# Attention's first group in small pieces: rows in two DMAs ahead of the weights, tiles from VectorE, rounding by halves

## What is computed

```python
def _layernorm(x, eps=1e-05):
    return (x - mean(x)) / sqrt(var(x) + eps)
def _rmsnorm(x, gamma):
    return x / max(norm(x), 1e-12) * 256 ** 0.5 * gamma
h = _rmsnorm(_layernorm(x), gamma)
q, kv, a = split(einsum('bnd,ed->bne', h, w_qkva), 3)    # w_qkva: 768 x 256
a = sigmoid(a)
y[t] = a[t] * y[t-1] + kv[t]                              # along the 1024 rows of a batch
x = x + q * y
x = x + moe(_layernorm(x))
```

## Time and profile before

| | us |
|---|---|
| median of 3 runs | 1058.49 |
| lowest, highest | 1057.33, 1059.9 |
| profiled execution, own time | 1060.74 |
| its span | 1059.0 |
| TensorE busy | 1011.7 (96%) |
| VectorE busy | 634.9 (60%) |
| ScalarE busy | 522.9 (49%) |
| GpSimd busy | 504.9 (48%) |

### The profile page before, as it was taken

The page is one execution under the profiler, slowest core; times in us unless marked ns, Lnnn a source line. Parts: engine busy times, 40 slices in busy tenths (PEclk is TensorE's granted clock), DMA queues, the critical chain, the costliest instruction groups (busy, mean ns, idle before and its releaser), DMA issues.

```text
span 1059.0 us, 20091 instructions
## 1 busy us (share of the span) xinstructions
PE 1011.7 (96%) x7277; PEld 955.5 (90%) x7277; DVE 634.9 (60%) x1094; ACT 522.9 (49%) x783; POOL 504.9 (48%) x285
## 2 busy tenths in 40 slices
PE   6999997999797699999999999999999999999998
PEld 5788997999797599999999999999999999999997
DVE  5997688775231365555555656555565556476766
ACT  3555431322131266666666766666666667423232
POOL 2226200000042277878787787878778776500000
PEclk9999998999898899999999999999999999999999
DMA  8333304004557567777777777777777777244231
GB/s 300 88 85 95 81 2 139 12 10 167 193 196 267 182 228 254 262 222 254 233 253 241 256 228 263 244 243 254 221 258 230 251 228 249 76 137 140 79 119 40
DMA packets 162219, 192.72 MB, mean 182 GB/s; under 512 B 76281, under 2 KB 147458, under 8 KB 151938
## 3 DMA queue, kind: packets, MB, share of 16 engines
q1 hardware_dynamic: 154656, 173.04, 50.4%
q0 software_dynamic: 6720, 18.36, 5.6%
q10 hardware_dynamic: 802, 0.79, 0.2%
HBM read 165.42 MB, written 26.74 MB: 181 GB/s over the span
## 4 chain that ended last, share of the span: by engine, by line
PE 86%; DVE 7%; DMA 3%; issue 2%; ACT 1%; POOL 0%; SPq 0%; DVEq 0%; POOLq 0%
PE ps L939 49%; PE ps L954 16%; PE ps L958 8%; PE ps L980 4%; PE ps L849 3%; PE ps L987 2%; DVE y_sb L1096 2%; PE ps L835 1%; DMA sorted_rows<-x_stage 1%; DVE hT_lo L1056 1%; DMA x_stage<-z_rows,idx_x 1%; PE ps L914 1%; PE ps L860 1%; DVE stats L1036 1%; DMA resid<-in_L_attn_x_dram 0%
## 5 line engine op out<-in xcount | busy, mean ns | idle before, releaser
L939 PE MATMUL ps<-xs_hi,w_both 128*128 128x256 f32 x3072 | 566.0, 284 | 8.3 <-DVE h_early L1378 7.5
L939 PEld LDWEIGHTS ps<-xs_hi,w_both 128*128 128x128 f32 x3072 | 480.6, 190 | 11.2 <-DVE h_early L1378 7.9
L939 PE MATMUL ps<-xs_lo,w_both 128*128 128x256 f32 x1536 | 435.8, 284 | 0.0
L551 POOL TENSOR_TENSOR w_both<-raw,w_both 128x2048 fp32r<-128x2048 f32 x65 | 307.9, 4737 | 94.2 <-ACT w_both L692 85.8
L939 PEld LDWEIGHTS ps<-xs_lo,w_both 128*128 128x128 f32 x1536 | 291.4, 190 | 0.1
L954 PE MATMUL ps<-w_both,h_hi 128*128 128x512 f32 x768 | 275.6, 401 | 6.7 <-DVE h_lo L1383 6.7
L958 PE MATMUL ps<-w_both,h_lo 128*128 128x256 f32 x768 | 216.6, 282 | 0.0
L733 ACT ACTIVATE silu<-ps 128x512 f32<-128x512 f32 x192 | 114.3, 595 | 205.3 <-PE ps L939 205.3
L1378 DVE TENSOR_TENSOR ps<-ps,silu 128x512 f32<-128x512 f32 x164 | 114.7, 699 | 127.1 <-ACT silu L733 120.2
L692 ACT ACTIVATE w_both<-raw 128x1024 fp32r<-128x1024 f32 x186 | 186.3, 1051 | 4.1 <-DMA raw<-in_L_ffn_w_up_dram 2.3
L954 PEld LDWEIGHTS ps<-w_both,h_hi 128*128 128x128 f32 x768 | 145.5, 189 | 40.9 <-DVE h_lo L1383 7.3
(11 more groups left out here) (184 smaller groups left out, 791.0 us busy)
## 6 DMA issues: line engine op xcount, KB each, us to landing
raw<-in_L_ffn_w_up_dram SPq DMA_DIRECT2D x33, 1024.0 KB, 5.3
raw<-in_L_ffn_w_gate_dram SPq DMA_DIRECT2D x33, 1024.0 KB, 6.9
raw<-in_L_ffn_w_down_dram SPq DMA_DIRECT2D x33, 1024.0 KB, 5.6
sorted_rows<-x_stage SPq DMA_DIRECT2D x32, 256.0 KB, 2.2
x_rows<-sorted_rows SPq DMA_DIRECT2D x128, 64.0 KB, 5.2
got<-expert_rows SPq DMA_DIRECT2D x32, 256.0 KB, 3.4
resid<-in_L_attn_x_dram SPq DMA_DIRECT2D x8, 512.0 KB, 6.6
z_rows<-z_all SPq DMA_DIRECT2D x8, 512.0 KB, 2.9
```

The lines of the kernel that those rows point to most:

```text
L551: pool.tensor_tensor(w_lo[buf][:, k, :], source[:, k, :], w_hi[buf][:, k, :].bitcast(F32), ALU.subtract).then_inc(wlo_ready[k], 1)
L939: last = pe.matmul(o, w[:, part, at[kd]:at[kd] + P], xx[:, u, kd, :], start=i == 0, stop=i == len(terms) - 1)
```

## The change

All of it lies before and in group 0 of attention.

- SP issues x of group 0 in two halves (two tiles each, `x_half`), then the weights in three parts (`w_in`, in the order 2, 1, 0), then x of groups 1 to 7 without a wait. ScalarE's queue keeps gamma and the router rows.
- TensorE does 14 of the warming transposes first, as soon as the identity is there, and 4 before the projection. In between it turns gamma and router, weight part 2, the four tiles of group 0 one by one as they come (`turn_first`), weight parts 1 and 0.
- GpSimd makes only the scales of group 0, no bias. VectorE makes the tiles of group 0 itself (`first_rows`: minus mean, times scale). 
- ScalarE does the first two steps of `prepare` for parts 2 and 1 (times gamma in two halves, rounding); VectorE keeps the subtraction (`prepare_lo`) and all of part 0.
- ScalarE rounds group 0's turned rows in two halves and VectorE makes their rests in two halves (`first_lo`); the first projection waits for the first half, and for the second only at its fourth term.
- VectorE takes group 1's `bn_stats` (`collect1`) before these and the `bn_aggr` and variances (`settle1`) after them.

The core of the diff:

```diff
@@ sync @@
-            for g in range(NC):
+            for half in range(2):
+                ts = slice(half * CT // 2, (half + 1) * CT // 2)
+                sp.dma_start(resid[:, ts, :], x_t[:, ts, :]).then_inc(x_half[half], 16)
+            w_v = w_qkva.rearrange("(e p) d -> p e d", p=P)
+            for part in PARTS:
+                es = slice(part * KD, (part + 1) * KD)
+                sp.dma_start(w_nat[:, es, :], w_v[:, es, :]).then_inc(w_in[part], 16)
+            for g in range(1, NC):
                 sp.dma_start(resid[:, g * CT:(g + 1) * CT, :], x_t[:, g * CT:(g + 1) * CT, :]
                              ).then_inc(x_in[g], 16)
-                if g == 0:
-                    sp.wait_ge(small_in, 48)
@@ gpsimd @@
                 pool.wait_ge(mv1_ready, g + 1)
+                if g == 0:
+                    pool.tensor_tensor(scale1[:, ts], var1[:, ts], power[:, :], ALU.pow).then_inc(scaled1, 1)
+                    return
@@ scalar @@
-            h_rows(0)
+            def prepare(nth, part):
+                if nth == 0:
+                    act.wait_ge(prep_done, 1)
+                act.wait_ge(prep, nth + 2)
+                for k in range(KD):
+                    last = act.activation(wT_32[:, part, k, :], ps[:, PART_BANKS[nth], k * D:(k + 1) * D],
+                                          ACT.Identity, scale=gT[:, k:k + 1])
+                last.then_inc(wT_scaled, 1)
+                act.wait_ge(wT_scaled, nth + 1)
+                act.activation(wT_hi[:, part, :, :], wT_32[:, part, :, :], ACT.Copy).then_inc(wT_rounded, 1)
...
-            h_hi_part(0)
+            prepare(0, PARTS[0])
+            act.wait_ge(hT_psum, 1)
+            act.activation(hT_hi[:, 0, 0, :], ps[:, 4, :], ACT.Copy).then_inc(hT_first_hi, 1)
+            act.activation(hT_hi[:, 0, 1, :], ps[:, 5, :], ACT.Copy).then_inc(hT_rounded, 1)
+            prepare(1, PARTS[1])
             h_rows(1)
@@ tensor @@
-            pe.wait_ge(small_in, 48)
+            for _ in range(WARM[0]):
+                pe.transpose(ps[:, 3, 0:P], ident[:, :], ident[:, :])
+            pe.wait_ge(small_in, 32)
...
+            def turn_first():
+                for k in range(CT):
+                    pe.wait_ge(h_first, k + 1)
+                    for kd in range(KD):
+                        last = pe.transpose(ps[:, 4 + kd, k * P:(k + 1) * P],
+                                            z_all[:, k, kd * P:(kd + 1) * P], ident[:, :])
+                last.then_inc(hT_psum, 1)
...
+                        if first and e == 0 and i == len(terms) // KD:
+                            pe.wait_ge(hT_split, 1)
...
-            turn_h(0)
-
-            for _ in range(WARM):
+            turn_w(PARTS[0], PART_BANKS[0])
+            turn_first()
+            turn_w(PARTS[1], PART_BANKS[1])
+            turn_w(PARTS[2], PART_BANKS[2])
+            for _ in range(WARM[1]):
                 pe.transpose(ps[:, 3, 0:P], ident[:, :], ident[:, :])
@@ vector @@
+            def first_rows():
+
+                dve.wait_ge(scaled1, 1)
+                for t in range(CT):
+                    dve.tensor_scalar(z_all[:, t, :], resid[:, t, :], mv1[:, t, 0:1], scale1[:, t:t + 1],
+                                      ALU.subtract, ALU.mult).then_inc(h_first, 1)
+
+            def first_lo(kd, rounded, signal):
+
+                dve.wait_ge(rounded, 1)
+                dve.tensor_tensor(hT_lo[:, 0, kd, :], ps[:, 4 + kd, :], hT_hi[:, 0, kd, :].bitcast(F32),
+                                  ALU.subtract).then_inc(signal, 1)
...
             dve.wait_ge(prep_done, 1)
-            prepare(0, PARTS[0])
-            prepare(1, PARTS[1])
-            h_lo_part(0)
-            statistics1(1)
+            first_rows()
+            collect1(1)
+            prepare_lo(0, PARTS[0])
+            first_lo(0, hT_first_hi, hT_first_lo)
+            first_lo(1, hT_rounded, hT_split)
+            settle1(1)
+            prepare_lo(1, PARTS[1])
             prepare(2, PARTS[2])
             statistics1(2)
```

More of the change, by code:

```diff
@@ L215, in preln_scan_moe_kernel @@
         x_in = [sem(f"x_in{g}") for g in range(NC)]
+        x_half = [sem("x_half0"), sem("x_half1")]
+        w_in = [sem(f"w_in{part}") for part in range(3)]
+        h_first = sem("h_first")
+        hT_first_hi, hT_first_lo = sem("hT_first_hi"), sem("hT_first_lo")
+        wT_scaled = sem("wT_scaled")
         small_in = sem("small_in")
@@ L224, in preln_scan_moe_kernel @@
         prep_done = sem("prep_done")
-        wT_made = sem("wT_made")
         wT_rounded = sem("wT_rounded")
@@ L284, in preln_scan_moe_kernel @@
         PART_BANKS = (0, 1, 6)
-        WARM = 18
+        WARM = (14, 4)
         R0 = SA + NS
@@ L619, in _ @@
             for k, (dst, src) in enumerate((
-                    (w_nat[:, :, :], w_qkva.rearrange("(e p) d -> p e d", p=P)),
                     (g_nat[:, :], gamma.rearrange("(k p) -> k p", p=P)),
@@ L798, in _, with turn_w @@
             last.then_inc(prep, 1)
-            for part, bank in zip(PARTS, PART_BANKS):
+            def turn_w(part, bank):
+                pe.wait_ge(w_in[part], 16)
                 for k in range(KD):
@@ L838, in route, with project @@
                 last.then_inc(lg_psum, 1)
-            def project(g, part, bank, signal):
+            def project(g, part, bank, signal, first=False):
                 c = g % 2
@@ L871, in _ @@
                 two = 6 - one
-                pe.wait_ge(hT_split, g + 1)
-                if g >= 1:
+                if g == 0:
+                    pe.wait_ge(hT_first_lo, 1)
+                    pe.wait_ge(wT_split, 1)
+                else:
+                    pe.wait_ge(hT_split, g + 1)
                     pe.wait_ge(y_ready, g)
-                if g == 0:
-                    pe.wait_ge(wT_split, 1)
-                project(g, 2, one, a_psum)
+                project(g, 2, one, a_psum, first=g == 0)
                 if g >= 1:
@@ L1030, in _, with collect @@
             step(dve.memset(keep[:, :, 0:1], 0.0))
-            def statistics(g, stats, mv, signal):
+            def collect(g, stats, signal):
                 if g >= 1:
@@ L1035, in statistics, with settle @@
                 for k in range(CT):
+                    if signal is mv1_taken and g == 0 and k % 2 == 0:
+                        dve.wait_ge(x_half[k // 2], 16)
                     last = dve.bn_stats(stats[:, k, :], resid[:, g * CT + k, :])
                 step(last)
+            def settle(g, stats, mv, signal):
                 for k in range(CT):
@@ L1041, in statistics, with collect1, settle1 @@
                 dve.wait_ge(signal, g + 1)
-            def statistics1(g):
-                dve.wait_ge(x_in[g], 16)
-                statistics(g, stats1, mv1, mv1_taken)
+            def statistics(g, stats, mv, signal):
+                collect(g, stats, signal)
+                settle(g, stats, mv, signal)
+            def collect1(g):
+                if g >= 1:
+                    dve.wait_ge(x_in[g], 16)
+                collect(g, stats1, mv1_taken)
+            def settle1(g):
+                settle(g, stats1, mv1, mv1_taken)
                 ts = slice(g * CT, (g + 1) * CT)
@@ L1051, in statistics1 @@
                                   ).then_inc(mv1_ready, 1)
+            def statistics1(g):
+                collect1(g)
+                settle1(g)
+            def first_rows():
[7 more added lines that the diff above has]
+                                  ALU.subtract).then_inc(signal, 1)
             def h_lo_part(g):
@@ L1129, in x_lo, with prepare_lo @@
                                   xs_hi[:, par, :, :].bitcast(F32), ALU.subtract).then_inc(x_split, 1)
+            def prepare_lo(nth, part):
+                dve.wait_ge(wT_rounded, nth + 1)
+                dve.tensor_tensor(wT_lo[:, part, :, :], wT_32[:, part, :, :],
+                                  wT_hi[:, part, :, :].bitcast(F32), ALU.subtract).then_inc(wT_split, 1)
             def prepare(nth, part):
@@ L1134, in prepare @@
                 turned = ps[:, PART_BANKS[nth], :].rearrange("p (k n) -> p k n", k=KD)
-                dve.tensor_tensor(wT_32[:, part, :, :], turned,
-                                  gT[:, :].unsqueeze(2).broadcast_to([P, KD, D]), ALU.mult
-                                  ).then_inc(wT_made, 1)
-                dve.wait_ge(wT_made, nth + 1)
+                step(dve.tensor_tensor(wT_32[:, part, :, :], turned,
+                                       gT[:, :].unsqueeze(2).broadcast_to([P, KD, D]), ALU.mult))
                 dve.tensor_copy(wT_hi[:, part, :, :], wT_32[:, part, :, :]).then_inc(wT_rounded, 1)
-                dve.wait_ge(wT_rounded, nth + 1)
-                dve.tensor_tensor(wT_lo[:, part, :, :], wT_32[:, part, :, :],
-                                  wT_hi[:, part, :, :].bitcast(F32), ALU.subtract).then_inc(wT_split, 1)
+                prepare_lo(nth, part)
             statistics1(0)
```

7 lines of the change are left out of this document (3 added, 4 removed).

## The result

| | before | after |
|---|---|---|
| median, us (8 runs each) | 1059.19 | 1054.74 |
| lowest to highest | 1057.33 to 1060.68 | 1053.92 to 1057.5 |
| profiled execution, own time | 1060.74 | 1054.47 |
| its span | 1059.0 | 1052.7 |
| first projection starts | 17.71 | 12.32 |

The account below looks back on a forecast made before the run. TensorE is busy for 96% of the span, so the change only shifts the first scan, set by a chain of waits: 6.4 us earlier, nothing behind it, giving 1052.1 us against the 1058.49 median; range 1050.3 to 1055.6.

Parts of the forecast that it names:

- (a): Loads, x ahead of the weights: group 0's halves at about 3.1 and 4.0 us, group 1's x by about 7.6.
- (b): Group 0's statistics on VectorE: GpSimd's power starts at 5.65 us and ends at 6.7.
- (c): TensorE's opening: fourteen warming transposes run until 6.2 us; VectorE's copy of gamma at 6.9.
- (d): Group 0's four tiles on VectorE: 0.25 us each in a row, at 7.4, 7.6, 7.9 and 8.1.
- (e): TensorE's turning: first weight part from 6.6 to 7.55 us, then eight tile transposes, hT_psum at 9.45.
- (g): TensorE before the first projection: clock up at 9.4 us, remaining transposes done at 10.7, hidden; kv at 16.4.
- (f): Rounding: ScalarE's first weight part from 7.7 us, 1.5 together; hT halves from 9.5; first projection at 10.85.
- (h): Group 1's chain: settle1 at 12.1, ScalarE's rows from 14.35, first scan at 17.45 instead of 23.89, 6.4 us earlier.
- (i): Everything behind the first scan: same instructions, costed at nothing, so the 6.4 us shift carries to the end.
- The late clock: TensorE's transposes and first projections stay at the lower level; scan at 20.6, -3.3, or 1055.2 us; chance 0.12.
- The slower case: TensorE's clock stays low through all of group 0, its 36 matmuls 8.3 longer: +2.8, or 1061.3 us; chance 0.05.
- No change: The shift is taken back behind attention by a wait not tied to attention's end: 1058.5 us; chance 0.08.

Follow-up runs that it names:

- e2: Changed kernel with x of group 1 issued behind the first part of the weights instead of all three; median 1053.82 us, ratio to before 0.995.
- e8: Changed kernel with group 0's tiles made on ScalarE again, with GpSimd's bias for them; median 1055.37 us.
- e11: Changed kernel with x of group 0 in one transfer of 512 KB instead of two of 256 KB; median 1054.96 us.
- e4: Changed kernel with group 1's bn_aggr and variances (settle1) right behind its bn_stats, ahead of wT_lo and hT_lo on VectorE; median 1056.73 us.
- e6: Changed kernel with settle1 first, as in e4, and 20 instead of 4 warming transposes before the first projection; median 1054.54 us.
- e5: Changed kernel with 20 instead of 4 warming transposes before the first projection; median 1054.91 us.
- e7: Changed kernel with x of group 1 behind the first weight part, settle1 first, and 20 warming transposes before the projection; median 1054.22 us.
- e9: e5's kernel with group 0's hT_hi and hT_lo each made at once instead of by halves; median 1055.9 us.
- e1: Kernel before with only the loads changed: x of group 0 in halves, weights in three parts, later x without a wait; median 1057.24 us.

## Why the prediction came out as it did

The direction, the last item of the chain (the sigmoid in front of the scan) and the way the shift carries through were right; the size was 6.4 for 4.45 us. The range held the time, but in part by luck: 1054.74 lies outside the bounds of my own case (1050.6 to 1053.9), and inside the range only because that was stretched to 1055.6 for a clock that comes late, which did not happen. Of the 2.6 us between 1052.1 and 1054.74, 1.95 is the size of the shift; the other 0.7 is the level it was taken from, the median of three runs (1058.49), where eight gave 1059.19. By the steps of the forecast:

- (a) x of group 0: statistics at 3.74, not 3.1, but all four without a gap, so the second half was there by 4.44. It cost nothing. **x of group 1 is the term that was wrong most**: forecast to land by 7.6 from the bandwidth alone, it landed at 9.51, 6.2 us after its issue, with other transfers in front and behind. VectorE took it up 1.43 later than forecast. The forecast called its earlier issue something that "nothing needs sooner", and did not see that its own new order puts this wait in front of wT_lo and hT_lo. e2 shows the price of the transfer: 0.9 us. The other 0.5 of the 1.43 is the tiles' (d), which would have come out had x been there.
- (b), (c) The power started at 6.12 and ended at 7.17, gamma's copy came at 7.04: as forecast within 0.5, and nearly equal, so that neither alone is worth moving.
- (d) Tiles 0.33 each, not 0.25, nearer to the 293 ns of the earlier trace rows than to what I took. By itself 0.5 up to 8.62; in this kernel hidden by the wait for x of group 1 (e8, e11).
- (e), (g) The level was up by 9.03, before the 9.4 of the forecast, and TensorE had hT_psum ready before ScalarE, which took the first half at 9.56 as forecast (9.5). The projection was 1.5 late (12.32 for 10.85), through VectorE alone.
- (f) ScalarE's part: 8.15 to 9.66 for the first weights, 1.5 as forecast, though 0.45 late; its first operation could still follow at once, at 9.56.
- (h) settle1 ended at 13.55, not 12.1 (the 1.4 of x). GpSimd then took 2.8 to the rows instead of 2.2: the second wrong term, 0.6, from VectorE's wT_lo beside it, which the forecast's own order of instructions placed there and whose effect on GpSimd it did not ask for. The trace of before had shown it, beside the wT_lo of 19.76:

```profile
19.93 0.58 POOL L532 TENSOR_TENSOR p_len<-mv,scale 128x4 f32<-128x4 f32 x1
```

The forecast's 2.05 from the power to the rows already held this 0.58; new was the power itself, 1.62 for 1.04. Together 2.0 at the rows (16.36 for 14.35) and 1.93 at the scan (19.38 for 17.45), which is the whole miss of the shift.
- (i) Right: 4.51 at the first scan, 4.45 at the end.

The rivals. The late clock did not happen in this kernel, but e4 shows that it stood half a microsecond of idle time away, and what it costs: 1.5 us at kv, 2.2 between the medians of e4 and e6. In e11, where TensorE waited 0.32 for the first tile, the level stayed low until 11.8, and the wait for x of group 1 hid it; but in e8 TensorE waited 0.69 at the same place and the level was up by 10.15, so that this wait is the cause is not shown. The slower case needs 24 low matmuls; e4 had about eight. "No change" fell with the scans. The chance given to a gain was right; what none of the cases held was a wait on the transfer of the next group.

## What to carry to other kernels

When work is pulled forward, cost the landing of every transfer that the new order waits for, with its queue in front of it, and not only that of the first one: here the next group's rows became the start of the chain (e2). Where an engine's new order puts operations beside another's short ones, look at which of them share a port; where it leaves TensorE idle for long right before its matmuls, fill that time (e6 against e4; filling the 1.8 us of the changed kernel brought nothing, e5). And read the marker at a second place: in e4, e6, e7 and e9 the last scan moved 0.35 less than the first, for a pause between them that the chain of the forecast did not hold.

One order stands untried, and the trace of the changed kernel suggests it. ScalarE idles for 4.35 us in front of group 1's rows, while the projection of a, which its sigmoid needs, is done by 14.95 + 0.39 = 15.34; yet the sigmoid stands behind the rows and releases the scan at 19.38. With the sigmoid first (about 1.0 us, so done when the rows can start) kv would end last. The scan started 0.51 behind the start of kv's last matmul in e6; from 17.66 that gives 18.17, an estimate of 1.2 us at the first scan. At the next projection it is at most 1.0, since TensorE is busy with q until 22.26 and now starts it at 23.23. No run shows it.

## What was not expected of the hardware

- x of group 1 landed 6.18 us after its issue with 1280 KB issued in front of it; with 768 KB in front (e2) it landed after 5.1.
- TensorE's level fell after 2.31 us of idling (e4), with five matmuls begun between 12.82 and 13.86 still fast in front of the fall; 1.82 us in the changed kernel did not bring it. Each is one profiled execution.
- A subtraction of 128x512 with two operands in SBUF on VectorE held up GpSimd's operations on 128x4: 1.62 for 1.02, 0.67 for 0.20, while bn_stats and a multiplication out of PSUM did not. The bias of the kernel before, 0.49 for 0.24, began 0.03 behind a cast of 128x512 from SBUF to SBUF and ended 0.09 behind its end; beside a multiplication out of PSUM (e1) it took 0.24.
- VectorE paused for 0.34 between the copy of the state and hT_lo in e4, e6, e7 and e9, with both operands there and no wait in the trace that releases it.
